# Self-attention: the next norm's statistics in the last quarter of their unit, its power, scaling and bias one unit later

## The reference

```python
x = _attn(_ln(x, g1, b1), _ln(x, g1, b1), Wq1, Wk1, Wv1, Wo1, bo1) + x   # self-attention
x = _attn(_ln(x, g2, b2), context, Wq2, Wk2, Wv2, Wo2, bo2) + x          # attention to 64 context tokens
x = _geglu_ff(_ln(x, g3, b3), Wp, bp, Wf, bf) + x
```

```python
def _ln(x, g, b):
    m = jnp.mean(x, axis=-1, keepdims=True)
    v = jnp.var(x, axis=-1, keepdims=True)
    return (x - m) * jax.lax.rsqrt(v + EPS) * g + b
```

## Time and profile before

| what | value |
|---|---|
| median of 3 runs | 2362.67 us |
| lowest and highest run | 2359.14 and 2363.01 us |
| the profiled execution, whole time | 2359.38 us |
| the profiled execution, span from first to last instruction | 2357.6 us |
| mean granted TensorE clock | 0.964 of full speed |
| busy share of the span | PE 91%, PEld 76%, DVE 69%, ACT 62%, POOL 47% |

### The profile page before, as it was taken

The page is one execution under the profiler, slowest core; times in us unless marked ns, Lnnn a source line. Parts: engine busy times, 40 slices in busy tenths (PEclk is TensorE's granted clock), DMA queues, the critical chain, the costliest instruction groups (busy, mean ns, idle before and its releaser), DMA issues. The chain is left out here.

```text
span 2357.6 us, 31301 instructions
## 1 busy us (share of the span) xinstructions
PE 2148.9 (91%) x11628; PEld 1790.6 (76%) x11628; DVE 1633.1 (69%) x2353; ACT 1450.3 (62%) x2098; POOL 1110.4 (47%) x867
## 2 busy tenths in 40 slices
PE   6967999997799999999999999999998799999998
PEld 4656878786677777777777777777776688899887
DVE  6566667664677777777777777777776776666554
ACT  5535666654477777777777777777775355455431
POOL 2144554543145454454444544445454566666432
PEclk7968999999899999999999999999999899999999
DMA  6710000011000000100001000000012411111000
GB/s 211 281 40 7 21 22 21 10 48 45 27 24 15 24 23 17 34 15 24 24 14 33 16 26 24 15 25 23 14 35 110 167 62 54 54 54 45 10 10 19
DMA packets 84280, 102.67 MB, mean 44 GB/s; under 512 B 29664, under 2 KB 61152, under 8 KB 83616
## 3 DMA queue, kind: packets, MB, share of 16 engines
q1 hardware_dynamic: 84128, 100.66, 12.8%
HBM read 65.50 MB, written 33.82 MB: 42 GB/s over the span
## 5 line engine op out<-in xcount | busy, mean ns | idle before, releaser
L146 PE MATMUL PS<-R 128*128 128x512 f32 (+1 forms) x2944 | 1035.0, 352 | 98.8 <-DVE R L162 57.8
L148 PE MATMUL PS<-R 128*128 128x512 f32 (+1 forms) x2944 | 1004.1, 341 | 0.0
L147 PE MATMUL PS<-R 128*128 128x512 f32 (+1 forms) x2944 | 1004.0, 341 | 0.0
L146 PEld LDWEIGHTS PS<-R 128*128 128x128 f32 x2944 | 571.3, 194 | 215.6 <-DVE R L162 72.8
L156 ACT ACTIVATE R<-PS 64x512 fp32r<-64x512 f32 (+4 forms) x860 | 460.5, 548 | 281.7 <-PE PS L1768 132.3
L148 PEld LDWEIGHTS PS<-R 128*128 128x128 f32 x2944 | 570.9, 194 | 61.9
L147 PEld LDWEIGHTS PS<-R 128*128 128x128 f32 x2944 | 573.0, 195 | 55.4
L162 DVE TENSOR_TENSOR R<-F,R 128x1024 fp32r<-128x1024 f32 (+2 forms) x416 | 479.2, 1157 | 45.5 <-POOL R L159 23.0
L159 POOL TENSOR_SCALAR R<-F 128x512 fp32r<-128x512 f32 (+1 forms) x343 | 296.9, 868 | 354.9 <-DVE F L1921 149.4
L1463 ACT ACTIVATE F<-PS 128x1024 f32<-128x1024 f32 x256 | 263.1, 1028 | 183.3 <-DVE R L162 138.8
L159 POOL TENSOR_SCALAR R<-R 64x512 fp32r<-64x512 f32 x128 | 142.4, 1127 | 403.2 <-ACT R L156 403.2
(11 more groups left out here) (90 smaller groups left out, 1989.6 us busy)
## 6 DMA issues: line engine op xcount, KB each, us to landing
F<-sd SPq DMA_DIRECT2D x128, 128.0 KB, 2.8
xs<-F SPq DMA_DIRECT2D x16, 512.0 KB, 2.6
F<-xs SPq DMA_DIRECT2D x16, 512.0 KB, 3.5
gd<-F SPq DMA_DIRECT2D x8, 768.0 KB, 3.6
vd<-F SPq DMA_DIRECT2D x8, 768.0 KB, 5.4
R<-gd SPq DMA_DIRECT2D x6, 1024.0 KB, 5.7
R<-vd SPq DMA_DIRECT2D x6, 1024.0 KB, 5.7
F<-in_x SPq DMA_DIRECT2D x8, 512.0 KB, 5.1
```

What stands on the lines that cost most here:

```text
L146: nc.tensor.matmul(o, L[0], Rr[0], start=start, stop=False, skip_group_check=share)
L147: nc.tensor.matmul(o, L[0], Rr[1], start=False, stop=False, skip_group_check=share)
L148: return nc.tensor.matmul(o, L[1], Rr[0], start=False, stop=stop, skip_group_check=share)
```

## The change

At `p = 4` the statistics stand behind quarter 3 instead of quarter 0. The power moves from quarter 0 of `p = 4` to quarter 0 of `p = 5`, and the scaling and the bias addition from the end of unit `p = 4` to the end of unit `p = 5`. No instruction is added or removed, and nothing changes on PE, ScalarE and SP.

```diff
@@ VectorE: dve_attention1
-                    if more and j == 0 and p == 4:
+                    if more and j == 3 and p == 4:
                         ln_x_stats(*after3(b))
...
-                if more and p == 4:
+                if more and p == 5:
                     ln_scale(18 + b, xbuf(*after3(b)), C)
@@ GpSimd: pool_attention1
-                    if more and j == 0 and p == 4:
+                    if more and j == 0 and p == 5:
                         ln_pool_rstd(18 + b)
...
-                if more and p == 4:
+                if more and p == 5:
                     ln_add(pool, *after3(b))
```

## The result

The changed kernel takes 2337.55 us (median of 4 runs, 2332.97 to 2338.70), beside 2361.24 us for the kernel before (4 runs, 2359.14 to 2363.01): a ratio of 0.9902, with a 95% interval of 0.9886 to 0.9919. The prediction was 2345 us with a range of 2339 to 2352. What follows asks two things: whether the 17.5 us came about as said, and where the other 6 are from.

A forecast was written before the change was run, and what follows sets the result against it. PE was taken to bound the self-attention, with VectorE's statistics making it wait at p = 4. 14.3 + 3.2 = 17.5 us off 2359.38 gives 2341.9, plus 3.3 for the median: 2345 us, range 2339 to 2352.

The forecast's parts named there:

- The statistics on the path: At p = 4, VectorE's statistics block delays PE by 1.79 us in each of eight units; moving it saves 14.3 us.
- The clock drops: Two p = 4 units at clock 0.92 lose their drops with the wait: 3.2 us; rival that drops stay or move, 0.20.
- The cover at the unit's end: At the end of p = 4, 2.05 us of statistics fit VectorE's idle time and cost nothing; uncovered, 16.4 us.
- The port: At p = 5, GpSimd's power beside VectorE's rest L162 costs nothing; rival that it holds the rest, 5.8 us, chance 0.10.
- The base: The median of before, 3.3 us above its profiled execution, was added to 2341.9 us, giving 2345 us.
- The range: From 2339 us, if part of the 3.3 us goes too, to 2352 us, covering staying clock drops and a held rest.

The follow-up runs named there:

- late_rest: Kernel before with only power, scaling and bias addition moved one unit later, statistics left at quarter 0 of p = 4: 1.0013 of before.
- stats_q2: Changed kernel with the statistics behind quarter 2 of p = 4 instead of quarter 3: 1.0037 of before.
- before_gate: Kernel before, with GpSimd's first bias addition (near 29 us) made to wait for VectorE's last rest of the first weights: 0.9971 of before.
- add_late: Kernel before with statistics and power in quarter 3 of p = 4, scaling at that unit's end, bias addition at the end of p = 5: 0.9924 of before.
- before_again: The kernel before, unchanged, timed and profiled a second time: 1.0009 of before.
- before_third: The kernel before, unchanged, timed and profiled a third time: 1.0009 of before.

## Why the prediction was right in its mechanism and wrong in its number

- **The statistics on the path** (14.3 us): right. With the statistics in quarter 0 (late_rest) or quarter 2 (stats_q2) PE waits for VectorE and the gain is gone, and in quarter 3 it is there; quarter 1 was not tried. Without a clock drop a p = 4 unit fell from 20.36 to 18.62 us in the mean, 13.9 us over eight.
- **The clock drops** (3.2 us): right. There were two in the p = 4 units of each profile of before (three in that of before_gate), and none in the 64 units of the eight profiles with the statistics in quarter 3, where no PE wait of a p = 4 unit is over 1.45 us. With the drops the p = 4 units save 17.1 us over three profiles each, beside 17.5.
- **The cover at the unit's end**: right, with 0.62 and 0.55 us left where 0.4 to 0.5 were expected. That the room reaches to the second L1530, about 4.1 us, was shown by add_late, which uses it up and pays 0.3 us a batch.
- **The port**: the value taken, nothing, was right for the power. But I weighed only this one pair. That the bias addition must end before VectorE's first 128x1024 rest, which the change respects with about 1 us to spare, is what makes moving it worth while, and I priced that row only by GpSimd's own queue.
- **The base**: this step failed, "The median of before lies 3.3 us above its profiled execution (2362.67), and the change touches nothing that I know to explain this, so I add it". The difference of 3.3 us was treated as a property of the kernel when it was scatter: in more runs the kernel before had medians of 2356.7 to 2361.1 us, around its profiled 2359.38, and reached from 2345.5 to 2367.1.
- **The range**: here the same step failed once more, the term of what lies outside the p = 4 units, and this is what left the result outside. The low end already had the 3.3 us taken off, "2341.9 less half of the spread of the runs, 3.9/2, rounded down", so down to 2339 it left about 3 us for all that lies outside the p = 4 units, and the median came 4.3 us below 2341.9. The profiled pair differs there by 26.4 - 16.9 = 9.5 us: 5.5 in front of the self-attention, 2.2 in its other units, 1.8 behind it. Three runs that lay within 3.9 us of each other did not show this; single runs reach some 10 us to each side of the median.

Is the surplus scatter, then? The changed kernel measured 0.9902, 0.9913 and 0.9930 of the kernel before in three comparisons, where the sum of 17.5 us gives 0.9926: inside the second and third interval, outside the first. Their mean is 0.9915, and the three intervals together leave it about 0.0012 to each side (my estimate), so 0.9926 lies at its edge. The start, 4.45 or 2.29 us in one row and 5.7 us at the ScalarE copies, is one cause of such differences that is shown, and it fell well for the changed kernel in the first two of its three profiles. That it fell so by luck is argued, not shown.

What stays open is why the bias row lands 3.0 us after its issue in some executions and 3.2 to 3.3 in others, which decides the start, and what the rest is: a mean ratio of 0.9915 is 20 us, of which the p = 4 units hold 17.1. The start, the clock drops between 80 and 640 us and waits for the small sum transfers (units of 18 to 21 us at the same place, p = 7 of the sixth batch, in profiles of both kernels) are candidates, of which only the start was tested.

## What to carry to other kernels

A block of side work in an in-order queue costs its full length in one place and nothing in another; look for the queue's idle row, whose releaser is another engine, and move the block right in front of it. Count what else may run there: a GpSimd instruction that reads SBUF and is shifted by a microsecond can hold a VectorE instruction of two SBUF inputs for nearly as long as it runs, here up to 2.2 of 2.5 us. And before a change of under 1% is predicted or judged, look how far repeated runs of the same kernel lie apart; three that agree do not tell it.

## What the runs showed of the hardware that was not expected

- The port is kept by whoever comes first: a difference of 0.2 to 0.3 us in a DMA's landing made a VectorE row 2.2 us longer, and a wait that takes the race away gained 6.8 us (0.9971, 0.9956 to 0.9986).
- An instruction that seems to be in the way can protect another one: the power in front of GpSimd's product kept it behind VectorE's rest, and moving it away made PE's wait 2.50 us instead of 1.82.
- GpSimd's power on 128x4 elements, 1.0 us long, holds nothing: the rests beside it took 1.21 and 1.22 us.
- PE's clock can fall to its lower level at single waits of 1.8 us between busy stretches: in nine of 32 like places over four profiles (before, before_again, before_third, before_gate), each time within about 1 us after the start of the matmuls that ended the wait. With waits of 2.4 to 3.1 us at another place it fell in six of eight (stats_q2), with 2.5 to 2.65 us at the first place in one of six (late_rest), and with waits of at most 1.45 us in none of 64. In the kernel before a drop made its unit 1.6 us longer, nearly as much as the wait itself.
